# One indirect gather of 1 KB rows per block in place of two of 512 B, in the first stage of a graph-attention and mixture-of-experts kernel

## The reference, cut to what matters

```python
def _L0_gnn_ref(x, edge_index, W, a_src, a_dst):
    src, dst = (edge_index[0], edge_index[1])
    h = jnp.einsum('ni,hio->hno', x, W)
    attn_src = jnp.einsum('hno,ho->hn', h, a_src[..., 0])
    attn_dst = jnp.einsum('hno,ho->hn', h, a_dst[..., 0])
    edge_attn = jax.nn.leaky_relu(attn_src[:, src] + attn_dst[:, dst], negative_slope=0.2)
    edge_attn_exp = jnp.exp(edge_attn - jnp.max(edge_attn))
    attn_sum = jax.ops.segment_sum(edge_attn_exp.T, dst, num_segments=N)
    attn_norm = edge_attn_exp / (attn_sum[dst].T + 1e-10)
    weighted_h = attn_norm[..., None] * h[:, src]
    out = jax.ops.segment_sum(weighted_h.transpose(1, 0, 2), dst, num_segments=N)
    return out.reshape(N, H * F_OUT) + x
...
x = x + _L0_gnn_ref(_layernorm(x), edge_index, W, a_src, a_dst)
x = x + _L0_ffn_ref(_layernorm(x)[None], gate_w, gate_b, w1, b1, w2, b2, gamma, beta)[0]
```

## Time and profile before the change

| | us |
|---|---|
| median of three runs | 1986.72 |
| the profiled execution, its own time | 1983.17 |
| its span, from the first instruction to the last | 1981.4 |

### The profile page before, as it was taken

One profiled execution on the slowest core, in us unless ns is written; L12 is line 12 of the kernel. 1 busy time (PEld: TensorE's weight loads), 2 busy tenths in 40 slices (PEclk: granted clock), 3 DMA queues, 4 the chain that ended last, 5 costly groups with the idle time before them and its releaser, 6 DMA issues.

```text
span 1981.4 us, 28027 instructions
## 1 busy us (share of the span) xinstructions
PE 1518.3 (77%) x6733; PEld 1113.7 (56%) x6733; DVE 1177.7 (59%) x3449; ACT 775.5 (39%) x2346; POOL 1213.1 (61%) x1197
## 2 busy tenths in 40 slices
PE   3927777777777777777777777673968999999975
PEld 2714444444444444444444444442848999999963
DVE  5746666666666666666666666668983444333338
ACT  2624444444444444444444444432622233223326
POOL 4066666666666666666666666645364776666757
PEclk9956666666666666766656666766559999999987
DMA  6544444444444444444444444432856878877876
GB/s 184 164 120 115 120 112 113 115 117 118 112 115 114 117 118 110 114 115 117 118 111 115 114 119 114 115 79 80 252 168 184 226 212 210 213 210 203 217 170 200
DMA packets 166686, 284.19 MB, mean 143 GB/s; under 512 B 31760, under 2 KB 93285, under 8 KB 166373
## 3 DMA queue, kind: packets, MB, share of 16 engines
q0 software_dynamic: 62256, 143.99, 30.5%
q1 hardware_dynamic: 101908, 137.90, 21.9%
q10 hardware_dynamic: 2368, 0.52, 0.2%
HBM read 240.97 MB, written 42.16 MB: 143 GB/s over the span
## 4 chain that ended last, share of the span: by engine, by line
PE 63%; DVE 18%; issue 8%; DVEq 3%; another core or an unknown queue 3%; POOL 2%; DMA 1%; ACT 1%; ACTq 0%; POOLq 0%; SPq 0%
PE bank L1057 29%; PE bank L1198 10%; PE bank L1210 10%; DVE region L1518 4%; PE bank L1046 3%; PE bank L1082 3%; PE bank L990 2%; DVE z L1471 2%; DVE region L1516 2%; DVEq L494 2%; PE bank L1043 2%; POOL region L925 1%; DVE z L1478 1%; DVE z L1483 1%
## 5 line engine op out<-in xcount | busy, mean ns | idle before, releaser
L895 POOL DMA_INDIRECT region<-node_rows,region x832 | 790.5, 950 | 483.7 <-issue 222.7
L1057 PE MATMUL bank<-region 128*128 128x264 f32 x1664 | 746.7, 597 | 84.5 <-DVE region L1518 81.3
L1057 PEld LDWEIGHTS bank<-region 128*128 128x128 f32 x1664 | 440.5, 290 | 224.2 <-issue 138.4
L1518 DVE TENSOR_TENSOR region<-region,bank 128x264 f32 x728 | 311.5, 428 | 354.3 <-PE bank L1057 269.0
L748 ACT ACTIVATE neg_max<-bank 128x1 f32<-128x1 f32 x104 | 17.8, 171 | 723.1 <-PE bank L1082 593.6
L1504 DVE TENSOR_TENSOR region<-region,bank 128x512 f32<-128x512 f32 x416 | 265.9, 681 | 7.2 <-ACT bank L755 4.8
L738 ACT ACTIVATE region<-iota_row,region 128x128 f32<-128x128 f32 x832 | 262.7, 386 | 0.0
L822 ACT ACTIVATE region<-bank,b_col 128x128 f32<-128x128 f32 x452 | 129.0, 368 | 311.6 <-PE bank L1198 210.6
L971 POOL DMA_INDIRECT sum_rows<-region,row_u x113 | 180.0, 1593 | 111.5 <-DVE region L1938 45.2
L1198 PEld LDWEIGHTS bank<-region 128*128 128x128 f32 x1808 | 220.1, 192 | 6.3 <-issue 0.4
L1198 PE MATMUL bank<-region 128*128 128x128 f32 x1808 | 220.7, 275 | 0.2 <-issue 0.2
(11 more groups left out here) (246 smaller groups left out, 1618.4 us busy)
## 6 DMA issues: line engine op xcount, KB each, us to landing
region<-in_L_ffn_w SPq DMA_DIRECT2D x129, 512.0 KB, 8.4
region<-dloc_rows SPq DMA_DIRECT2D x104, 256.0 KB
region<-node_rows,region POOLq DMA_INDIRECT x832
node_rows<-region SPq DMA_DIRECT2D x12, 528.0 KB
y_rows<-region SPq DMA_DIRECT2D x7, 896.0 KB, 5.5
sum_rows<-region SPq DMA_DIRECT2D x7, 896.0 KB, 7.7
region<-in_x SPq DMA_DIRECT2D x5, 896.0 KB, 12.4
region<-sum_rows SPq DMA_DIRECT2D x5, 896.0 KB, 11.1
```

The costliest lines, as they stand in the source:

```text
L895: p.indirect_dma_start(gathered[g % SLOTS][:, j, :], None, node_rows, bass.IndirectOffsetOnAxis(src_idx[:, k:k + 1], 0)).then_inc(row_in[g ...
L1057: pe.matmul(bank[AGG_BANKS[k % AGG]][:, 0:ROW], onehot[:, (g % 3) * GROUP + j, :], gathered[g % SLOTS][:, j, :], start=True, stop=True).th ...
L1518: v.tensor_tensor(rows, rows, new, ALU.add).then_inc(acc_add)
```

## The change

`src_pad` and `dst_pad` give way to one table in HBM, `edge_rows`, of 782 x 2 x 128 int32: a chunk's 128 sources and its 128 destinations are one row of 1024 B. SP writes it by six DMAs in place of four: for each of the two inputs one of 781 pieces of 512 B and one of 128 B for the last, partly filled chunk, and two that fill that chunk up. POOL's `fetch` issues one gather of 1024 B rows per block. The number of rows in a gather, 128, stays. DVE's wait on a block is for one gather. Every other instruction stays in its place; the semaphore `edge_rows_in` takes the place of two, and lines after L76 are one number lower up to the changed DMAs.

```diff
-        src_pad = dram("src_pad", [CHUNKS * P], I32)
-        dst_pad = dram("dst_pad", [CHUNKS * P], I32)
+        edge_rows = dram("edge_rows", [CHUNKS, 2, P], I32)
...
-            d.dma_start(dst_pad[0:EDGES].rearrange("(a b) -> a b", a=16),
-                        dst.rearrange("(a b) -> a b", a=16)).then_inc(dst_pad_in, 16)
-            d.dma_start(src_pad[0:EDGES].rearrange("(a b) -> a b", a=16),
-                        src.rearrange("(a b) -> a b", a=16)).then_inc(src_pad_in, 16)
+            whole = EDGES // P
+            for n, ends in enumerate((src, dst)):
+                d.dma_start(edge_rows[0:whole, n, :],
+                            ends[0:whole * P].rearrange("(c e) -> c e", e=P)).then_inc(edge_rows_in, 16)
+                d.dma_start(edge_rows[whole:whole + 1, n, 0:P - tail],
+                            ends[whole * P:EDGES].rearrange("(a n) -> a n", a=1)).then_inc(edge_rows_in, 16)
             d.wait_ge(pool_consts, POOL_CONSTS["pad"])
-            d.dma_start(src_pad[EDGES:].rearrange("(a n) -> a n", a=1), pad_i[:, 0:tail]).then_inc(src_pad_in, 16)
-            d.dma_start(dst_pad[EDGES:].rearrange("(a n) -> a n", a=1), pad_i[:, P:P + tail]).then_inc(dst_pad_in, 16)
+            for n in range(2):
+                d.dma_start(edge_rows[whole:whole + 1, n, P - tail:P], pad_i[:, n * P:n * P + tail]).then_inc(edge_rows_in, 16)
...
             def fetch(b):
-                for n, table in enumerate((src_pad, dst_pad)):
-                    p.indirect_dma_start(rows_i[:, 2 * b + n, :], None, table.rearrange("(c e) -> c e", e=P),
-                                         bass.IndirectOffsetOnAxis(step_ci[:, b:b + 1], 0)).then_inc(rows_in[b], 16)
+                p.indirect_dma_start(rows_i[:, 2 * b:2 * b + 2, :].rearrange("p n e -> p (n e)"), None,
+                                     edge_rows.rearrange("c n e -> c (n e)"),
+                                     bass.IndirectOffsetOnAxis(step_ci[:, b:b + 1], 0)).then_inc(rows_in[b], 16)
             p.wait_ge(table_step, TABLE["step_ci"])
-            p.wait_ge(src_pad_in, 32)
-            p.wait_ge(dst_pad_in, 32)
+            p.wait_ge(edge_rows_in, 96)
...
-                    v.wait_ge(rows_in[b], 32)
+                    v.wait_ge(rows_in[b], 16)
```

More of the change, by code:

```diff
@@ L263, in build_program @@
         bank = [ctx.enter_context(nc.psum_tensor(f"bank{i}", [P, 512], F32)) for i in range(8)]
-        dst_pad_in, src_pad_in, ends_in = sem("dst_pad_in"), sem("src_pad_in"), sem("ends_in")
+        edge_rows_in, ends_in = sem("edge_rows_in"), sem("ends_in")
         w_gnn_in, gate_in, b1_in = sem("w_gnn_in"), sem("gate_in"), sem("b1_in")
```

## The result

The changed kernel took 1976.65 us (median of 5 runs, 1973.58 to 1980.63), the kernel before 1985.87 us beside it (5 runs): a ratio of 0.9956, 95% interval 0.9945 to 0.9966. So it is faster, by 9.2 us between the medians; 11.4 were predicted. The profiled execution took 1973.58 us with a span of 1971.8, against 1983.17 and 1981.4.

The account below looks back on a forecast made before the run. The prediction took the first stage as bound by PE's signals arriving late behind a backlog of POOL's gathers. Terms 11.4 + 0 + 0 us off 1986.72 gave 1975.3 us, range 1971.5 to 1983.0.

Parts of the forecast that it names:

- The issue of seven gathers: On POOL in the first stage: seven fewer issues save 8.8 us there, worth nothing to the total by themselves.
- The backlog of 1.45 us per gather: Downstream of POOL: each 128-row gather delays PE's signals about 1.45 us, rows counting; seven end at 40.15 instead of 50.17.
- it does not go by bytes: First-stage gathers: row size hardly counts; the opposing rival, 1 KB rows leaving 2.9 us each, meant 1986.7 us, chance 5%.
- The 11.4 us: PE's first-stage path: the fourth pair of L1018 starts at 45.6 instead of 57.03, the whole forecast gain.
- I take the clock as staying up: PE around the transposes: only 0.2 us without work, so its clock stays 1.00 from 38 to 56 us.
- the 0.6 us for its normalising: PE's fourth pair of L1018: DVE must normalise that tile first, so 45.6 us instead of PE's own 45.0.
- It lasts: From 56 us on PE alone paces; none of the 11.4 us is given back, first L895 moving from 99.73 to 88.3.
- The pieces: SP's copies: 1562 pieces of 512 B at 28 ns, 2.7 us per engine, 0.5 more than before, covered by 2.8.
- Two further DMA issues on SP cost it a microsecond or so: On SP: two more issues cost about a microsecond, nothing overall, since SP waits 18.1 us for ACT afterwards.
- the sign that I had named: DVE idle before its statistics at 20.46, released by a load of `x`, would show the copies' costing wrong.
- The attention vectors: POOL starts at 15.92 on their landing, sharing engines with SP's copies: effect taken as 0, with 2.2 us either side.
- The rival that the hole is not the gathers' doing: First stage, ACT's 10.99 us wait from 39.19: PE's transposes may themselves finish slowly; time stays at 1986.7 us, chance 9%.

Follow-up runs that it names:

- the fast chip: The changed kernel, unaltered, in a set of runs where the kernel before takes 1778.36 us: 1779.54 us, ratio 1.0010.
- the deferred kernel: The changed kernel with later gathers spaced behind node tiles, one `x` load before SP's copies, another and the copies after the chunk table's load: 1781.21 us, 1.0017 of before.

## Why the prediction was right, and where it was not

The direction and the mechanism held. By its own steps:

1. The issue of seven gathers is worth nothing by itself. Right: on the fast chip, where the issue is all there is to save, POOL idles 41.53 us before its first L895 with fourteen gathers and 48.67 with seven, and the change gains nothing. (The equal ends of the stage, 89.79 and 89.75, are partly chance, as said above.)
2. The backlog of 1.45 us per gather: `tile_row` at 42.40, where 32.12 + 7 x 1.45 gives 42.27. It agrees, but does not test it, since PE had issued its seventh transpose only a little earlier. The test is the kernels with fourteen gathers: 1.43 and 1.44 us per gather to ACT's release in the one from the new table and the one with added gathers of 32 rows; in the one with 128 rows the release is not as clean, but the stage ends as late. That it does not go by bytes was right; that rows count was wrong. What the step lacked was the condition: it holds on a chip whose loop takes 1.45 to 1.47 us per gather, and on one with 1.25 there is no backlog.
3. The 11.4 us is the term that was mis-sized. The pair of L1018 that began at 57.03 begins at 48.56, not at 45.6: **8.5 us** gained, 2.9 less. The L990 put at 40.6 is the second one behind the transposes, and it began at 44.23, one L1018 and one L990 behind the row at 43.10: 3.6 us late. PE started 2.1 us late (37.34 in place of 35.21), and with the fallen clock the way from L1018 to L1002 took 3.88 us (37.34 to 41.22) in place of 2.33 (35.21 to 37.54), 1.55 more; together 3.7. "I take the clock as staying up" was wrong. By then DVE was far enough ahead that the 0.6 us for its normalising, in the sum, did not come, which leaves 3.0. The release, at 42.3, was no longer what bound PE. On the fast chip the same kernel kept its clock (37.39 to 39.72, 2.33), so the 1.55 us are not a fixed cost of the change.
4. It lasts, nearly: a store of `node_rows` held ACT for 1.05 us at 60.09, and 7.8 us arrive at the first L895. The loop's groups of 11.75 us are as before. Some 1.8 us more are gained later, half in the loop and half behind it, for which I have no cause; the runs of one kernel scatter by 7 us.
5. The pieces were sized rightly: 1562 of them, 28.4 ns on average (28 taken), 2.8 us per engine if all 16 shared them and 4.0 if 11 did. Which it was, no run settles: in the deferred kernel, where these pieces ran alone from 31 to 32 us, they filled 79.6% of the 16 engines' time. The step failed in "Two further DMA issues on SP cost it a microsecond or so", which it put at nothing. Those two are the L538, and they stood 6.21 and 3.03 us behind the copies of 781 pieces. I had costed the pieces on the DMA engines and not on the queue that issues them. The loads of `x` went out at 15.03, and DVE stood 1.77 us for one at 20.67, the sign that I had named. I had also not looked at what those loads meet in their new place: the round trip of `chunk_rows`, which starts 1.65 us earlier (16.98, before 18.63) and ends 2.1 us later (DVE's L1321 at 28.55, before 26.43). Issuing the loads first does not mend it, as the run shows.
6. The attention vectors: POOL starts at 14.28 in place of 15.92, 1.6 us earlier, inside the 2.2 us that the step kept. It is eaten by the round trip.

So the time came out 1.4 us above the forecast, nearer than its parts deserve, and that is luck: the first stage gained 7.8 us and not 11.4; 1.8 came later for a reason that I don't have, and the median of before was 0.9 lower in this set of runs.

The rival that the hole is not the gathers' doing stood on the Trainium skill (SBUF - State Buffer, the section on the two separate sides): PE waits on no one, and DMA cannot slow compute. On the fast chip the trace agrees with it, tile for tile, through fourteen gathers. On the slow ones PE's signals are late, by up to 10.9 us (the last transpose ended at 39.2 us and `tfirst` began at 50.17). That is no contention of ports, of which the section speaks, so the rule could not rule the hole out.

## What to carry to other kernels

Where PE's consumers wait for matmuls that were issued long ago, look at what POOL issues meanwhile: back-to-back gathers were priced here by their number, from 32 rows of 128 B to 128 rows of 1056 B, so make fewer and larger ones or draw them apart, but put each where its rows are still early for the engine that runs furthest ahead. Cost a copy in many pieces on the queue that issues it too, and then look at what goes out behind it and which small round trip it will meet. And a gain that hangs on such a wait is to be measured in more than one set of runs: here it is 9.2 us of 1986 in one and nothing of 1778 in another.

## What the runs showed of the hardware

- One program takes 1778 to 1780 us in some sets of runs and 1973 to 1986 in others. The difference lies mostly in the loop of gathers, 1.250 us each against 1.454 to 1.471, while the gather's own time on POOL is 945 to 948 ns in both. Whether the chip or its state sets it, and what part PE's clock has in it, is open.
- On slow chips, seven gathers of 128 rows of 1 KB with seven of 32 rows of 128 B between them held PE's signals for 1.44 us per gather, fourteen of 128 rows of 512 B for 1.43 and 1.44. The signals are not all held to the end: seven of fourteen were through by 43.8 us in the kernel before, the last at 50.2.
- The issue behind a copy of 781 pieces stood on SP for 6.21 and 3.03 us in the changed kernel, for 3.82 and 1.66 us in the one with the loads first, and for 1.11 and 1.90 us in the deferred one, where SP had been waiting before.
- PE's idle stretch of 3.15 us was followed by a clock of 0.72 from 38 to 44 us, and in the kernel before one of 2.98 us by 1.00. On the fast chip one of 3.07 us was followed by 1.00 (the changed kernel), and one of 2.33 us by 0.89 (the kernel before). So it is not the length of the stretch alone; what it is these traces do not show.
